# Mixture-of-experts stage: shared gate and up products halved over two expert steps, splits on ScalarE and VectorE reordered

## What is computed

```
x = x + attention(layernorm(x), ctx) @ wo.T
scores = softmax(xf @ gate_w.T); topk_w, topk_idx = top_k(scores, 6)
gx = xp[buf_tok]                                   # 64 experts x 128 rows x 512
gu = einsum('ech,ehi->eci', gx, gate_up_proj)      # 512 -> 2 * 192
hid = silu(g) * u
eo = einsum('eci,eih->ech', hid, down_proj) * buf_w
routed = zeros.at[buf_tok].add(eo)
shared = silu(xf @ shared_gate_w.T) * (xf @ shared_up_w.T) @ shared_down_w.T
```

## Time and profile before

| | us |
|---|---|
| median of three runs | 871.37 (868.22 to 872.88) |
| the profiled execution, its own time | 869.38 |
| its span on the core | 867.7 |
| TensorE busy | 772.4 (89%) |
| VectorE busy | 594.7 (69%) |
| ScalarE busy | 446.4 (51%) |
| expert steps: first down product to last | 481.02 to 832.32 |

### The profile page before, as it was taken

One profiled execution on the slowest core, in us unless ns is written; L12 is line 12 of the kernel. 1 busy time (PEld: TensorE's weight loads), 2 busy tenths in 40 slices (PEclk: granted clock), 3 DMA queues, 4 the chain that ended last, 5 costly groups with the idle time before them and its releaser, 6 DMA issues.

```text
span 867.7 us, 11717 instructions
## 1 busy us (share of the span) xinstructions
PE 772.4 (89%) x3862; PEld 649.4 (75%) x3862; DVE 594.7 (69%) x1168; ACT 446.4 (51%) x798; POOL 323.2 (37%) x256
## 2 busy tenths in 40 slices
PE   3999999899998999999988899998999989999930
PEld 2888877778776887788877788877888877888820
DVE  5426576575675755774596988887888878888820
ACT  3324323333232423243243888787777877778820
POOL 1001010553106520075103565456555666555630
PEclk8999999999999999999999999999999999999965
DMA  6851253322622217202727999999999999999968
GB/s 204 278 193 49 97 195 145 99 79 80 232 95 99 97 61 277 98 31 84 282 94 227 296 325 308 329 322 320 320 312 312 314 308 321 300 303 304 262 83 176
DMA packets 69158, 180.31 MB, mean 208 GB/s; under 512 B 10144, under 2 KB 10528, under 8 KB 64416
## 3 DMA queue, kind: packets, MB, share of 16 engines
q1 hardware_dynamic: 49632, 137.65, 45.4%
q0 software_dynamic: 19472, 42.02, 21.8%
HBM read 143.33 MB, written 44.97 MB: 217 GB/s over the span
## 4 chain that ended last, share of the span: by engine, by line
PE 52%; DVE 15%; DMA 10%; issue 8%; ACT 8%; POOL 4%; SPq 1%; DVEq 0%; ACTq 0%; POOLq 0%
PE bank L1066 8%; PE bank L1068 8%; PE bank L1067 8%; DMA xg<-x_rows,idx_all 3%; DMA stage<-wvT_in 3%; PE ps_gu L1068 2%; PE ps_gu L1066 2%; PE ps_gu L1067 2%; ACT gu_hi L1304 2%; PE ps_xgT L1503 2%; PE scores L1066 2%; PE scores L1068 2%; PE scores L1067 2%; DVE xn L808 2%; DVE xgT_lo L1385 2%
## 5 line engine op out<-in xcount | busy, mean ns | idle before, releaser
L1385 DVE TENSOR_TENSOR gu_lo<-gu_raw,gu_hi 128x768 fp32r<-128x768 f32 x128 | 122.1, 956 | 35.9 <-ACT gu_hi L1304 32.5
L413 POOL DMA_INDIRECT table<-rows,slot x72 | 81.0, 1126 | 138.8 <-DVEq L822 118.0
L1304 ACT ACTIVATE gu_hi<-gu_raw 128x768 fp32r<-128x768 f32 x128 | 107.5, 843 | 12.0 <-PE bank L1068 8.9
L1263 POOL DMA_INDIRECT xg<-x_rows,idx_all x64 | 82.4, 1288 | 53.2 <-DVEq L659 28.6
L1066 PE MATMUL ps_gu<-gu_hi,xgT_hi 128*128 128x384 f32 x256 | 91.5, 357 | 0.0
L1068 PE MATMUL ps_gu<-gu_hi,xgT_lo 128*128 128x384 f32 x256 | 86.5, 338 | 0.0
L1067 PE MATMUL ps_gu<-gu_lo,xgT_hi 128*128 128x384 f32 x256 | 86.5, 338 | 0.0
L442 ACT ACTIVATE qT_hi<-bank 128x512 fp32r<-128x512 f32 x32 | 19.2, 599 | 117.3 <-PE bank L1068 117.3
L1503 PE MATMUL ps_xgT<-ident,xg 128*128 128x128 f32 x256 | 39.5, 277 | 27.2 <-DVE xgT_lo L1385 20.2
L447 ACT ACTIVATE pbuf<-scores,negmax 128x1024 f32<-128x1024 f32 x16 | 17.9, 1116 | 86.5 <-DVE negmax L593 86.5
L1503 PEld LDWEIGHTS ps_xgT<-ident,xg 128*128 128x128 f32 x256 | 29.1, 141 | 38.5 <-issue 27.5
(11 more groups left out here) (257 smaller groups left out, 2250.8 us busy)
## 6 DMA issues: line engine op xcount, KB each, us to landing
gu_raw<-gate_up_in SPq DMA_DIRECT2D x128, 384.0 KB, 9.0
dn_raw<-down_in SPq DMA_DIRECT2D x64, 256.0 KB, 5.7
dn_raw<-down_in SPq DMA_DIRECT2D x64, 128.0 KB, 9.3
x_rows<-pbuf SPq DMA_DIRECT2D x17, 256.0 KB, 2.1
stage<-wqT_in SPq DMA_DIRECT2D x4, 1024.0 KB, 4.8
stage<-wkT_in SPq DMA_DIRECT2D x4, 1024.0 KB, 4.8
stage<-ctxT_in SPq DMA_DIRECT2D x4, 1024.0 KB, 5.5
stage<-wvT_in SPq DMA_DIRECT2D x4, 1024.0 KB, 8.9
```

The costliest lines, as they stand in the source:

```text
L413: pool.indirect_dma_start(out=table, out_offset=bass.IndirectOffsetOnAxis(ap=slot[:, i, k:k + 1], axis=0), in_=rows[:, i, k, :], in_offset ...
L1263: pool.indirect_dma_start(out=xg[:, e % 3, :], out_offset=None, in_=x2_rows, in_offset=index(("expert", e))).then_inc(gathered[e % 3], 16)
L1304: act.activation(gu[n % RING][0][:, half(part)], gu_raw[:, n % RING, half(part)], ACT.Copy).then_inc(weights_high, 1)
L1385: return dve.tensor_tensor(lo, x, hi.bitcast(F32), ALU.subtract)
```

## The change

Three things change, and no arithmetic is added or removed.

1. A gate or up event is cut in two: the first six matmuls (chunks 0 and 1 of four) stay in the even step, the last six go to the odd step after it. Down events stay whole. ScalarE and VectorE handle a gate's or an up's output one step later than before.
2. The order of ScalarE's and VectorE's work inside a step changes. ScalarE makes xgT right after silu, and only then splits the second half of the gate/up weights and the down weights. VectorE splits the second half of gate/up of e+3 and the down weights of e+2 at the start of its step, before hidT_lo.
3. Down weights move one step ahead in `PIECES`, and so on ScalarE: it splits the down weights of e+3 in step e, no longer those of e+2. SyncE loads them one expert further ahead.

```diff
-EVENT_AT = {2 * k: event for k, event in enumerate(shared_events())}
+EVENT_AT, BEGUN_AT = {}, {}
+for _k, _event in enumerate(shared_events()):
+    EVENT_AT[2 * _k + (_event[0] != "down")] = _event
+    if _event[0] != "down":
+        BEGUN_AT[2 * _k] = _event
...
-          ("dn", 1, 0), ("gu", 3, 0), ("gu", 3, 1)]
+          ("dn", 1, 0), ("gu", 3, 0), ("gu", 3, 1), ("dn", 2, 0)]
...
-    PIECES += [("dn", _e + 2, 0)] if _e + 2 < E else []
+    PIECES += [("dn", _e + 3, 0)] if _e + 3 < E else []
...
@@ sync
+        load_dn(sp, 5)
         for e in range(E):
-            if e == FILLED_LAST["up", 5] + 1:
+            if e == EVENT_STEP["up", 5] + 1:
...
-            if e + 5 < E:
-                load_dn(sp, e + 5)
+            if e + 6 < E:
+                load_dn(sp, e + 6)
@@ scalar, step(e)
             if e + 4 < E:
-                act_weights(act, mine[0], mine[0] + 1)
+                act_weights(act, PIECE_NO["gu", e + 4, 0], PIECE_NO["gu", e + 4, 0] + 1)
             if e + 2 < E:
                 gate(e + 2)
-                act_weights(act, mine[-1] - (1 if e + 4 < E else 0), mine[-1] + 1)
+            if e + 4 < E:
+                high_xgT(e + 4)
             if kind == "up":
                 act_high(act, n)
             if e + 4 < E:
-                high_xgT(e + 4)
+                act_weights(act, PIECE_NO["gu", e + 4, 1], PIECE_NO["gu", e + 4, 1] + 1)
+            if e + 3 < E:
+                act_weights(act, PIECE_NO["dn", e + 3, 0], PIECE_NO["dn", e + 3, 0] + 1)
@@ vector, step(e)
             if kind == "up":
                 dve_hid(dve, n)
+            if e + 3 < E:
+                dve_weights(dve, PIECE_NO["gu", e + 3, 1], PIECE_NO["gu", e + 3, 1] + 1)
+            if e + 2 < E:
+                dve_weights(dve, PIECE_NO["dn", e + 2, 0], PIECE_NO["dn", e + 2, 0] + 1)
             if e + 1 < E:
                 low_hidT(e + 1)
...
             if e + 2 < E:
                 up(e + 2)
-                dve_weights(dve, mine[-1] - (1 if e + 4 < E else 0), mine[-1] + 1)
+            if e + 4 < E:
+                low_xgT(dve, e + 4)
             if kind == "up":
                 dve_low(dve, n)
-            if e + 4 < E:
-                low_xgT(dve, e + 4)
@@ tensor
-        for c in range(C):
+        for c in range(*chunks):
...
+            (kind, n), chunks = (None, None), (0, C // 2)
+            if e in BEGUN_AT:
+                kind, n = BEGUN_AT[e]
+            elif e in EVENT_AT:
+                (kind, n), chunks = EVENT_AT[e], (C // 2, C)
```

More of the change, by code:

```diff
@@ L1091, in shared_events @@
     return [e for e in events if e[0] != "down" or e[1] not in TILES_OF[0][:LEAD_TILES]]
-EVENT_AT = {2 * k: event for k, event in enumerate(shared_events())}
+EVENT_AT, BEGUN_AT = {}, {}
[3 more added lines that the diff above has]
+        BEGUN_AT[2 * _k] = _event
 assert max(EVENT_AT) < E - 2
-FILLED_LAST = {("up", n): 2 * k for k, (kind, n) in enumerate(shared_events()) if kind == "up"}
+EVENT_STEP = {event: step for step, event in EVENT_AT.items()}
 SETS = [("shared", tile) for tile in TILES_OF[0][:LEAD_TILES]]
@@ L1356, in scalar @@
         high_hidT(0)
-        act_weights(act, 7, 10)
+        act_weights(act, 7, LEAD)
         def step(e):
@@ L1366, in step @@
                 high_hidT(e + 1)
-            if e == 3:
+            if (kind, n) == ("down", TILES_OF[0][-1]):
                 act_high(act, 3)
             out_rows(("expert", e))
-            mine = [PIECE_NO[p] for p in (("gu", e + 4, 0), ("gu", e + 4, 1), ("dn", e + 2, 0)) if p in PIECE_NO]
             if e + 4 < E:
-                act_weights(act, mine[0], mine[0] + 1)
+                act_weights(act, PIECE_NO["gu", e + 4, 0], PIECE_NO["gu", e + 4, 0] + 1)
             if e + 2 < E:
                 gate(e + 2)
-                act_weights(act, mine[-1] - (1 if e + 4 < E else 0), mine[-1] + 1)
+            if e + 4 < E:
+                high_xgT(e + 4)
             if kind == "up":
@@ L1440, in vector @@
         low_hidT(0)
-        dve_weights(dve, 7, 10)
+        dve_weights(dve, 7, PIECE_NO["gu", 3, 0] + 1)
         def step(e):
@@ L1446, in step, with pe_half @@
                 dve_hid(dve, n)
+            if e + 3 < E:
+                dve_weights(dve, PIECE_NO["gu", e + 3, 1], PIECE_NO["gu", e + 3, 1] + 1)
+            if e + 2 < E:
+                dve_weights(dve, PIECE_NO["dn", e + 2, 0], PIECE_NO["dn", e + 2, 0] + 1)
             if e + 1 < E:
                 low_hidT(e + 1)
-            if e == 3:
+            if (kind, n) == ("down", TILES_OF[0][-1]):
                 dve_low(dve, 3)
-            mine = [PIECE_NO[p] for p in (("gu", e + 4, 0), ("gu", e + 4, 1), ("dn", e + 2, 0)) if p in PIECE_NO]
             if e + 4 < E:
-                dve_weights(dve, mine[0], mine[0] + 1)
+                dve_weights(dve, PIECE_NO["gu", e + 4, 0], PIECE_NO["gu", e + 4, 0] + 1)
             if e + 2 < E:
                 up(e + 2)
-                dve_weights(dve, mine[-1] - (1 if e + 4 < E else 0), mine[-1] + 1)
+            if e + 4 < E:
+                low_xgT(dve, e + 4)
             if kind == "up":
                 dve_low(dve, n)
-            if e + 4 < E:
-                low_xgT(dve, e + 4)
         for e in range(E):
             step(e)
-    def pe_half(pe, n, side, full):
+    def pe_half(pe, n, side, full, chunks=(0, C)):
         b, m = PAIRS[n]
@@ L1468, in pe_half @@
         out = pair_banks(n)[:, side, :]
-        if side == 0:
+        if side == 0 and chunks[0] == 0:
             if b != B - 1 and m == 0:
@@ L1474, in pe_half, with pe_gate, pe_up @@
         w = (kept.sg, kept.su)[side]
-        for c in range(C):
+        for c in range(*chunks):
             last = product(pe, out, [h[:, c * SI + m * P:c * SI + (m + 1) * P] for h in w],
                            [h[:, c, :] for h in x], c == 0, c == C - 1)
[L1478 to L1484, removed]
+        if chunks[1] == C:
+            last.then_inc(full, 1)
+    def pe_gate(pe, n, chunks=(0, C)):
+        pe_half(pe, n, 0, sgate_full, chunks)
+    def pe_up(pe, n, chunks=(0, C)):
+        pe_half(pe, n, 1, sup_full, chunks)
     def shared_down(pe, tile):
```

5 lines of the change are left out of this document (2 added, 3 removed).

## The result

The changed kernel takes 867.54 us (median of 20 runs, 863.39 to 869.89), the kernel before 869.15 us (20 runs, 866.04 to 872.88). The ratio is 0.9970, with a 95% interval of 0.9956 to 0.9984: faster, by 2.6 us of 869 as the ratio has it (the medians differ by 1.6), and less than the 0.5% from which the prediction calls a change a change. The forecast was 7.4 us less.

A forecast was written before the change was run, and what follows sets the result against it. Uneven steps make TensorE wait on VectorE beside a full DMA, which then paces the new kernel. Savings of 9.2 and 0.9 less 2.7 give 7.4 us: profiled 869.4 becomes 862.0, median 864, range 858 to 868.

The forecast's parts named there:

- the 9.2 of the prediction: Steps 4 to 59: us saved, 310.0 against 319.2, from bytes needed per phase over a DMA rate, with corrections.
- The order costed at nothing: VectorE's reordered splits: xgT_lo waits of 1.1 to 1.4 us go; hidT_lo comes later, still in time, at no cost.
- The new wait at steps 12, 32 and 52: TensorE waits 2.2 us for pT_lo at each batch's first down event, hidden under DMA time, else at most 6.6 dearer.
- The rate of 322 GB/s: DMA rate assumed for the expert stage, the mean by length of 320 and 327 from two stretches.
- DMA paces: First rival: transfers pace the new kernel's expert stage; 864 us, between 858 and 868; chance 0.50.
- The prediction's floors: TensorE's least time per phase in steps 4 to 59, 291.7 us in all, including the new pT_lo wait.
- Steps 0 to 3: Start of the expert stage: 20.5 us before against 19.6 after, 0.9 saved.
- The shallower prefetch: Two thirds of the weights are landed 4 us less ahead, giving back 2.7 us at the start.
- The signs: Expected in the profile: xgT_lo waits near zero, even steps of 5.2 to 5.4, weights awaited 10 us, over 317 GB/s.
- Room in the transfers: Second rival: DMA share over 1 is overlap, so TensorE's floors of 291.7 us hold; 843 us; chance 0.10.
- the adds pace: Third rival: chained adds pace the down phases, 49 us each if an add takes 9.5; 866 to 874; chance 0.27.
- ScalarE holding the weights back: Fourth rival: late gathers delay ScalarE's weight splits and so refills; slower, 876 us or more; chance 0.13.

The follow-up runs named there:

- e7: The kernel before with the second 128 KB part of each down load fetched for the first three experts only (7.3 MB less); 900.07 us, ratio 0.9908.
- e6: The changed kernel with the second 128 KB part of each down load fetched for the first three experts only (7.3 MB less); 891.11 us, ratio 0.9832.
- e11: Changed kernel with pT of each batch's last up event early, 7.3 MB fewer down weights, and shared rows added into their own tensor; 838.10 us, ratio 0.9646.
- e5: The changed kernel measured again, unaltered, on another chip; 907.49 us against 908.95 for the kernel before, ratio 0.9988.
- e1: The changed kernel with gate and up events whole again, keeping the new order and down weights a step ahead; 904.30 us, ratio 0.9946.
- e2: The kernel before with only the gate and up events halved, in the old order; 910.57 us against 910.85, ratio 1.0015.
- e3: The changed kernel with both pT halves of each batch's last up event made early in the step; 905.01 us against 910.85, ratio 0.9945.
- e8: The changed kernel with pT of each batch's last up event early and 7.3 MB fewer down weights; 887.77 us, ratio 0.9767.
- e4: The changed kernel with shared rows added into a third tensor in a chain of their own; 907.47 us against 910.85, ratio 0.9975.
- e10: The changed kernel with pT of each batch's last up event early and the shared activations' reload moved to steps 24 and 28; 864.63 us, ratio 0.9948.

## Why the prediction was right or wrong

**The number.** 867.5 lies inside the range of 858 to 868, and barely. Part of that is luck: the forecast started from a median of 871.4 over three runs, and over 20 runs it is 869.2. From 871.4 the measured ratio of 0.9970 would have given 868.8, outside the range. The gain was put at 7.4 us and is 2.6. The prediction gave 0.70 to faster by over 0.5% and 0.18 to within it, and within it is what came.

**What bounds the kernel.** Both parts of the reading held. The dependence problem is real: with the bytes off, e7 and e6 differ by 8.9 us in the stage. That this is near the 9.2 of the prediction is chance, since the 9.2 was worked out from bytes and a rate, and e6 has 12.3 us of other waits in place of the 17.8 on xgT_lo. With those gone too, e11's stage is 20.3 us shorter than e7's. The full DMA system beside it is real too: taking 7.3 MB off sped up both kernels, the one before by 0.9%, and the changed one by 1.6% (0.9832 for 0.9988).

**The order costed at nothing, the waits on xgT_lo gone.** Right for xgT_lo: 18.1 us to none. Not quite for hidT_lo, where the prediction had a cover of 0.4 to 1.6 us and no cost: TensorE waits 1.7 us for it once in the result, 2.6 in e5. Gate and up steps take 5.28 each for a forecast of 5.24. What the prediction did not see is that this came from the order more than from the halves (e1 has it without halves; e2, with halves alone, kept 5.3 us of it and got nothing for it). With whole events and the new order the kernel is as fast as any.

**The new wait at steps 12, 32 and 52.** Its size and place were right: 2.2 forecast, 6.1 us in three waits measured (6.6 in e5). Its cost was not. The prediction had it "hidden under the DMA's time in all three places, and at most 3 x 2.2 = 6.6 dearer were it not". Taking it away (e3) gives 0.9945, where the changed kernel has 0.9970 and 0.9988 in its two measurements: 2.2 to 3.9 us, a third to over a half of the bound. Only the larger of the two is clear of the noise; with fewer bytes the same edit takes 3.3 us off the stage (e6 to e8). While TensorE stands there, GpSimd and ScalarE have nothing to hand on, and what they would have asked of the DMA comes later; a full DMA hides a wait only where the queue of requests doesn't run short because of it. These last two sentences are argued from the rates of e3 and e5 (315 and 311 GB/s with the same bytes), not shown by themselves.

**The rate of 322 GB/s.** This is the term of the sum that was mis-sized, and the prediction named it as its weakest step. The bytes were right: the changed kernel moved 317.3 us x 314 GB/s = 99.6 MB, where the table has 100.8 needed. At 322 GB/s these take 309.5 us, where the forecast had 310.0, and the stage took 7.3 us more. 320 and 327 were the rates of stretches of 70 and 30 us picked where the DMA was fullest. Over its whole stage the kernel before had moved 312 GB/s, and no kernel with all its bytes passed 317, also where ScalarE waited 20.9 to 38.5 us for weights (311 in e4 and e5, 315 in e3, 317 in e1). By phases the rate of 327 came once, in steps 12 to 19 with the reload, where the forecast of 49.4 us stands against 48.8; the two long gate/up phases ran at 315 and 313, and took 67.5 for 65.1.

A rate over the stage is only its bytes over its time, so it doesn't say by itself what held the stage up. TensorE's waits do. In the result they are 19.2 us, and four stretches of 3.41 us at half the clock cost up to 6.8 more (an estimate, half of each stretch). With the 288.3 of the floor that makes 314.3 of the 317.3. The prediction reckoned neither with the clock nor with longer waits on gathered rows; it expected weights to be late, and in this execution ScalarE waited only 3.0 us for them, of which 1.7 reached TensorE. So DMA paces is right in that fewer bytes make it faster, but in the result it reached TensorE mostly by the gathers, which wait in GpSimd's order behind the adds. Why no kernel passed 317 stays open. It is not the chain of adds alone, since without it (e4) the rate was 311, and it is no fixed ceiling of the traffic, since e11 moves 316 GB/s with only 4.2 us of waits on weights. The prediction's floors were a little low as well: without the 6.6 us of the new wait they sum to 285.1, where e11 shows 288.3.

By the figure of the Trainium skill that the prediction set against the rows (DMA: Bandwidth & Descriptors, section Bandwidth, some 425 GB/s for a core that loads alone) the transfers would not bind. The experiments with fewer bytes show that they do in part, at 311 to 317 GB/s with this mix of weights, gathers and adds.

**Steps 0 to 3.** 0.9 us were to be saved. In the profiled execution of the result they took 21.4 us for 20.5 before, at a granted clock of 0.92:

```profile
476.34:497.75 21.41, 21.41 (x110) 19.20 (x111) 19.43 (x32) 18.41 (x35) 9.28 (x6) 0.92 1.02 309
```

Without the drop of the clock, in e5, they took 19.9, near the 19.6 of the forecast.

**The shallower prefetch.** 2.7 us were to be given back at the start. No run tells this term apart. ScalarE waited 4.8 us for weights in the stage of before, and 3.0 and 20.9 us in the two profiled executions of the changed kernel.

**The signs.** The waits on xgT_lo are gone and the new wait at steps 12, 32 and 52 is there, as named. Most gate and up steps take 5.28, but the first two or three of each of these phases take 5.3 to 9.0, with the waits on gathered rows. Weights awaited for 10 us or more came in one of two executions. A rate over 317 GB/s came in neither (314 and 311).

**The rivals.** DMA paces, the first, is the nearest to what happened, with the reservations above. Room in the transfers is out for these kernels; e11, in which both bytes and chain are off, comes to 292.8, near the 291.7 that this rival worked with, but e11 has no waits on pT_lo, of which the 291.7 hold 6.6. That the adds pace was half right: in the down phases it did not bind (45.7 and 43.5 us where the rival had 49), and GpSimd's waits on its own adds in the two long gate/up phases are 9.6 and 9.3 us where they were 9.5 and 9.0, so they are no sign of it either; yet it is what comes next as soon as the bytes allow. ScalarE holding the weights back: the wait that this rival needs is there, since ScalarE waits 10.2 us for the transposed rows (ps_xgT) in the stage of the result, a wait that the same stretch of before doesn't have. What it costs was not taken apart; it doesn't make the kernel slower, as the ratio is under 1. In e5 two of SyncE's issues behind the reload take 1.59 and 1.76 us where others take 0.33 and 0.47, so refills were late there too, and not only by a wait of ScalarE.

**What stays open.** The stage varies by 4.4 us between the two profiled executions of the changed kernel (317.3 and 321.75). TensorE's waits for hid, 4.4 us in e5 and not in the list of the result, are of that size, and they follow weights that come late. Why they come late in one execution and not in the other was not found out. A direct comparison of e1, e3 and the changed kernel in the same rounds was not made; the three stand against the kernel before. e1, e3 and e10 beat the kernel before by 0.5%; against the changed kernel they are ahead clear of noise only where e5 stands for it.

## What to carry to other kernels

When removing a dependence wait would make a full DMA system the bound, take its rate from the whole stage and not from the fullest stretch: 322 for the 312 to 314 of the stage is the size of the gain that was missed here. Don't cost a new wait at nothing because a transfer is the bound: three of them, 6.1 us in all, cost 2.2 to 3.9 here. And where two pacers may stand behind each other, take one off by an experiment that leaves work out: fewer bytes in both kernels (e6, e7) showed what the dependences cost, and the same edit with the adds' chain off (e11) what the chain would cost next.

## What the runs showed of the hardware

**The clock of TensorE fell behind some single waits of 1.7 to 2.3 us, and not behind others of the same length.** In the stage of the kernel before, with 25 waits of 1.4 us at most on xgT_lo and six of 1.7 at most on gathered rows, the granted clock is 1.00 in every window of the earlier trace rows. In the changed kernel it fell to half four times in the same stretch, for 3.41 us each time. The window around the wait on pT_lo at step 12, the one behind it, and the next:

```profile
544.95:548.35 3.40, 1.37 (x10) 1.10 (x9) 3.37 (x8) 2.90 (x6) 1.57 (x1) 1.00 1.08 295
548.35:551.76 3.41, 3.41 (x9) 2.67 (x10) 2.07 (x3) 0.74 (x2) 0.00 (x0) 0.50 1.06 329
551.76:555.17 3.41, 3.41 (x20) 3.10 (x19) 0.42 (x1) 2.24 (x4) 1.56 (x1) 1.00 1.06 378
```

TensorE was busy for 1.37 of 3.40 us, and then had a clock of 0.50 while it worked without a gap. Matmuls of 512 columns start 0.43 us apart there and 0.23 to 0.24 elsewhere. The Trainium skill, TensorE: Matmul & The Clock Gate, Part 1, has two levels, 1.2 and 2.4 GHz, and 427 and 216 ns between such matmuls. The rows agree with the first; at the full clock they lie 15 to 25 ns above the second. The same follows a wait on gathered rows, before a drop that starts at 715.60:

```profile
715.28 0.85 PE L1513 MATMUL ps_xgT<-ident,xg 128*128 128x128 f32 x4 [2.14 <-DMA xg<-x_rows,idx_all]
```

The other two drops follow waits of 1.67 us (from 579.07) and 2.29 us (from 602.96). But the wait on pT_lo at step 32 was as long as that at step 12, and behind it the matmuls start 0.24 us apart, at the full clock:

```profile
664.57 0.50 PE L1066 MATMUL ps_dn<-xnT_hi,pT_hi 128*128 128x512 f32 x1 [2.03 <-DVE pT_lo L1392]
...
665.15 0.40 PE L1068 MATMUL ps_dn<-xnT_hi,pT_lo 128*128 128x512 f32 x1
665.39 0.40 PE L1066 MATMUL ps_dn<-xnT_hi,pT_hi 128*128 128x512 f32 x1
```

In all, seven waits of the stage last 1.6 to 2.3 us, and four of them have a drop behind them.

As far as these rows show, a wait of 2 us at one place can cost more than its length, and more than two of 1.1 in different steps. In 3.41 us at half the clock some 1.7 us of work are lost. But the drops did not decide between the kernels: e3 has the lower mean clock in its stage (0.97 against 0.99 in e5) and the better time. That the DMA leaves slack for some of it would fit, and is not shown.

**An add into rows of DRAM takes about 8.3 us to land while the DMA is full.** The median from issue to landing, 560 to 630 in the changed kernel, is 7.9 to 8.4 for the four kinds of add, one of them here:

```profile
second_sum<-eo,idx_all POOLq DMA_INDIRECT x4, 8.4
```

Three adds into the same tensor in the timeline of GpSimd in the changed kernel, the last two started as soon as the one before had landed:

```profile
580.85 1.69 POOL L1276 DMA_INDIRECT second_sum<-eo,idx_all  x1 [3.80 <-DMA second_sum<-product,idx_all]
...
589.41 1.57 POOL L1276 DMA_INDIRECT second_sum<-product,idx_all  x1 [1.69 <-DMA second_sum<-eo,idx_all]
...
597.93 1.68 POOL L1276 DMA_INDIRECT second_sum<-eo,idx_all  x1 [2.06 <-DMA second_sum<-product,idx_all]
```

They stand 8.56 and 8.52 apart. That is the pace of a chain of adds here, and a third tensor was worth 8.1 us of the stage once the bytes were off (e8 to e11), and nothing before (e4).
